# Context weights loaded one pair earlier, context projections ahead of the output blocks, and the gate's steps spread over later blocks

## The chip, the cores and the metric

The kernel runs on one core of a Trainium2 chip. The metric is the device time of one execution in microseconds; the time before is the median of three runs.

## The reference, cut to what matters

```
x = x + attn(layernorm(x))      # 16 heads of 64, causal, w_qkv and w_out
x = x + xattn(layernorm(x), ctx)
x = x + ffn(layernorm(x))       # x: 4 x 1024 x 1024, ctx: 4 x 1024 x 512
# xattn: query = ctx Wq^T + bq, key = ctx Wk^T + bk   (128 wide)
#        attention = softmax(query key^T);  x_m[l, m] = sum_n x[l, n] attention[m, n]
# ffn:   8 experts; u = select_weight . (x - mean_diff) / norm, score = sum u^2
#        gate = sigmoid(slope (score - center)); scale, index = max, argmax over the experts
#        out = (1 - scale) x + scale (bias[index] + degen[index] (update[index] . (x - debias[index])))
```

## The kernel before, in words

The batch has four sequences of 1024 rows. Each is done in eight head pairs, so there are 32 pairs n = 0 to 31 in one long software pipeline. Every 32-bit product is built out of three 16-bit products (high by high, high by low, low by high), which is why nearly each value has a high part, rounded on GpSimd or ScalarE, and a low part, made on VectorE. A row block is 128 rows, so a sequence has eight of them, 0 to 7.

The order of the work is written out by hand: for each engine there is a list of steps for a plain pair (PE_BODY and so on) and one for the last pair of a sequence (PE_TAIL and so on), which also carries everything that isn't attention. Every engine walks its own list in order, and a step that has to wait holds up all that stands behind it. A "+" behind a step means that it belongs to the next pair, or, for steps that aren't of a pair, to the next sequence; "-" means the pair before. The steps that matter here, with their lines:

- Attention of a pair. P (PE, L532 to L534): projections, four parts for each half of q, k and v. CH, CL (ACT L726, DVE L813): high and low part of a projection. S q (PE, L577): scores of row block q. X q (DVE, L846 to L853): row maxima. E q j (ACT, L739): exponential for head j. R q (DVE, L859, L862): reciprocal of the sum. H q j (POOL, L1077) and L q j (DVE, L813): high and low part of the probabilities. T q (SP, L418): DMA transpose of row block q, after L q 1. V (SP, L423): transpose of v. M g (PE, L602): probabilities times v for half g; M1 of a pair runs in the list of the next pair. OH, OL: high and low part of its result.
- Output projection. OI i (SP, L480): loads a quarter of w_out, 1 MB, into the room of the normalized x. B i h (PE): half h of output block i; B00 waits for all four OI of the sequence, B10 for RA0. RI i (SP, L499): x for the residual. RA i (DVE, L1040): adds the residual.
- Context. KI (SP, L485): the 512 KB of context weights, which go into the room of the attention weights. KH, KL (ACT L759, DVE L1005): their high and low part. JI i (SP, L491), JH i, JL i (ACT L766, DVE L1009): a quarter of the context and its two parts, through one buffer. G i (PE): its query and key; QH i, QL i (ACT L772, DVE L1018): the two parts of the result. N i, CX, CE, CR, CHI, CLO, CT: context scores, softmax and transpose.
- Cross attention and the gate, for row block i. LX, LH, LL, LT: second layer norm, its parts, its transpose. Z i h (PE): half h of x times attention. XB i (DVE, L1050): adds it. TB i (DVE, L818): statistics of the third norm; TS, TX, TH, TL, TT: that norm (ACT L797), its parts (DVE L1057) and transpose. F i (PE): gate and low-rank products. GA i (DVE, L936 to L950, 12 small instructions): scores of the experts. GE i (ACT, L801): exponential. GB i (DVE, L955 to L968, 8 small instructions and one over the whole block): choice of the expert, and the block scaled. D i (PE, L694), WHI i, WLO i (ACT L806, DVE L1064): transpose and parts of the low-rank row. U i (PE): up projection. Y i (DVE, L1069): sum; YO i (SP, L520): store.
- AI, AB, AS, AX, AH, AL, AT: first layer norm of the next sequence, between the steps of the gate.

The waits that the change touches or meets: F i waits for GB i-1 (the semaphore f_g, L687), D i for GB i, U i for WLO i and Y i-1, TX i for GB i-2 (two buffers of the normalized block, xn3), Z i for XB i-2, M1 of the last pair of a sequence for QL3 (L597), G 0 for KL and JL0, E of the first pair of a sequence for the last Y, H q for the transpose of q-2 (pn has two buffers), T0 to T3 for M1 of the pair before.

Of the kernel before, what the change touches and what calls it, by code (L numbers as in the profile page):

```python
# [137 lines left out]
def decoder_layer(nc, x, w_qkv, w_out, ctx_t, w_ctx, b_ctx, w_ffn, v_ffn, w_up, center, slope, out):  # L138
    es = ExitStack()
    with es:  # L140
# [66 lines left out]
        with ExitStack() as s1:  # L207
            sel_u = sb(s1, "sel_u", [P, EXPERTS * SEL])
            sel_sq = sb(s1, "sel_sq", [P, EXPERTS * SEL])
            g8 = sb(s1, "g8", [P, 12, EXPERTS])  # L210
            g1 = sb(s1, "g1", [P, 8])
# [999 lines left out]
```

## Time and profile before

| | |
|---|---|
| median of 3 runs | 2787.72 us (2785.35 to 2791.86) |
| the profiled execution | 2785.46 us, of which the span is 2783.6 us |
| TensorE (PE) busy | 2415.4 us, 87% of the span |
| VectorE (DVE) busy | 1877.4 us, 67% |
| ScalarE (ACT), GpSimd (POOL) busy | 783.4 us, 711.4 us |
| share of the chain that ended last | PE 52%, DVE 22%, DMA 12% |

TensorE is busy for most of the span. Times in rows are microseconds from the start of the span. In a row of the timeline the brackets say how long the engine was idle before the row, and what released it. The stretch from 1173.7 to 1497.5 is the list of the last pair of the second sequence (pair 15); the three other sequences have the same one, and that of the last sequence has no next sequence in it.

### The profile page before, as it was taken

What the parts mean: (1) busy time and instruction counts of PE and PEld (TensorE: products, weight loads), DVE (VectorE), ACT (ScalarE), POOL (GpSimd) and SP (SyncE); (2) the same over time, 40 slices, a digit from 0 to 9 for tenths busy, and PEclk for the clock granted to TensorE, in tenths of its full rate; (3) what the DMA queues carried; (4) which work ended last, traced back from release to release, by engine and by line L of the source; (5) the groups of instructions that cost most, each with busy time, mean ns of one, the idle gap of its engine ahead of it and who ended that gap; (6) DMA issues with size and microseconds to landing.
All of it is one profiled execution on the core that took longest, in us unless ns stands there. A gap on an engine that the chain in (4) does not pass through costs nothing.

```text
span 2783.6 us, 37859 instructions
## 1 busy us (share of the span) xinstructions
PE 2415.4 (87%) x14389; PEld 1187.7 (43%) x14389; DVE 1877.4 (67%) x3421; ACT 783.4 (28%) x1557; POOL 711.4 (26%) x981
## 2 busy tenths in 40 slices
PE   0588889699889999879979999979989999978996
PEld 0233444344444444445444444444444444434453
DVE  4577877646866767755785777765685777765566
ACT  1033333322213333321212333332211343332110
POOL 3123433214311222212421222212430222221220
PEclk9899999899999999989999999989989999998997
DMA  6678788857636776785654777776663677775543
GB/s 178 214 174 184 164 208 181 204 126 151 141 94 126 141 150 135 136 213 120 137 115 105 153 135 146 143 183 138 143 142 88 133 142 143 143 156 145 106 84 83
DMA packets 986009, 403.97 MB, mean 145 GB/s; under 512 B 937116, under 2 KB 946332, under 8 KB 985828
## 3 DMA queue, kind: packets, MB, share of 16 engines
q1 hardware_dynamic: 985828, 401.56, 65.3%
q8 instruction: 114, 1.87, 0.3%
q14 instruction: 67, 0.55, 0.1%
HBM read 133.05 MB, written 33.55 MB: 60 GB/s over the span
## 4 chain that ended last, share of the span: by engine, by line
PE 52%; DVE 22%; DMA 12%; issue 5%; ACT 4%; POOL 3%; SPq 2%; ACTq 0%; POOLq 0%; DVEq 0%
PE ps_p L532 8%; PE ps_p L534 8%; PE ps_p L533 8%; DMA r<-pn 7%; PE ps_s L532 5%; PE ps_s L533 5%; PE ps_s L534 5%; PE ps_s L577 5%; DVE pn L813 4%; PE ps_o L602 4%; DVE peak L850 3%; ACT probs L739 2%; DMA qk<-in_x 2%; DVE bn L818 2%; PE ps_s L582 1%
## 5 line engine op out<-in xcount | busy, mean ns | idle before, releaser
L1077 POOL TENSOR_SCALAR pn<-probs,rden 128x640 f16<-128x640 f32 (+7 forms) x512 | 386.6, 767 | 1297.0 <-DVE rden L862 830.4
L739 ACT ACTIVATE probs<-ps_s,low,back 128x640 f32<-128x640 f32 (+7 forms) x512 | 421.3, 826 | 859.0 <-DVE low L853 747.7
L813 DVE SCALAR_TENSOR_TENSOR pn<-probs,rden,pn 128x640 f16<-128x640 f32 (+7 forms) x512 | 473.9, 958 | 159.7 <-POOL pn L1077 159.5
L532 PE MATMUL ps_p<-r,w 128*128 128x512 f16 x1344 | 513.1, 382 | 3.3 <-DVE qk L813 3.3
L533 PE MATMUL ps_p<-r,w 128*128 128x512 f16 x1344 | 512.1, 381 | 0.0
L534 PE MATMUL ps_p<-r,w 128*128 128x512 f16 x1344 | 511.9, 381 | 0.0
L577 PE MATMUL ps_s<-qk 64*128 64x512 f16 (+3 forms) x2304 | 242.1, 336 | 129.5 <-ACT probs L739 122.8
L850 DVE TENSOR_REDUCE peak<-ps_s 128x2 f32<-128x1280 f32 (+3 forms) x128 | 241.3, 1885 | 36.6 <-PE ps_s L582 33.9
L602 PE MATMUL ps_o<-r,vn 128*64 128x512 f16 (+3 forms) x2304 | 212.2, 340 | 36.7 <-issue 36.1
L532 PE MATMUL ps_s<-r,pn 128*128 128x512 f16 x512 | 200.1, 391 | 11.0 <-DMA pn<-pn 11.0
L577 PEld LDWEIGHTS ps_s<-qk 64*128 64x128 f16 x2304 | 91.0, 96 | 274.0 <-ACT probs L739 171.6
L534 PEld LDWEIGHTS ps_p<-r,w 128*128 128x128 f16 x1344 | 132.2, 98 | 160.8 <-issue 4.2
L533 PE MATMUL ps_s<-r,pn 128*128 128x512 f16 x512 | 199.1, 389 | 0.0
L534 PE MATMUL ps_s<-r,pn 128*128 128x512 f16 x512 | 198.3, 387 | 0.0
L602 PEld LDWEIGHTS ps_o<-r,vn 128*64 128x64 f16 x2304 | 140.4, 114 | 125.2 <-issue 73.8
L532 PEld LDWEIGHTS ps_p<-r,w 128*128 128x128 f16 x1344 | 132.4, 99 | 141.8 <-DVE qk L813 5.3
L533 PEld LDWEIGHTS ps_p<-r,w 128*128 128x128 f16 x1344 | 132.4, 99 | 136.4 <-issue 2.5
L1081 POOL TENSOR_SCALAR ve<-mv 128x1 f32<-128x1 f32 x96 | 31.0, 323 | 473.0 <-DVE mv L821 471.5
L532 PE MATMUL ps_s<-r 128*128 128x512 f16 x384 | 145.9, 380 | 0.0
L533 PE MATMUL ps_s<-r 128*128 128x512 f16 x384 | 145.5, 379 | 0.0
L534 PE MATMUL ps_s<-r 128*128 128x512 f16 x384 | 145.5, 379 | 0.0
L859 DVE TENSOR_SCALAR den_s<-den 128x2 f32<-128x2 f32 x256 | 42.9, 167 | 133.9 <-ACT probs L739 133.6
(163 smaller groups left out, 3545.7 us busy)
## 6 DMA issues: line engine op xcount, KB each, us to landing
w<-w_pairs SPq DMA_DIRECT2D x72, 512.0 KB, 4.0
qk<-in_x SPq DMA_DIRECT2D x32, 512.0 KB, 4.2
r<-wo_pairs SPq DMA_DIRECT2D x16, 1024.0 KB, 6.1
w_raw<-in_x SPq DMA_DIRECT2D x32, 512.0 KB, 4.7
out<-r SPq DMA_DIRECT2D x32, 512.0 KB, 2.9
r<-in_w_qkv SPq DMA_DIRECT2D x24, 512.0 KB, 5.6
w_raw<-in_w_qkv SPq DMA_DIRECT2D x24, 512.0 KB, 5.7
w_pairs<-w SPq DMA_DIRECT2D x24, 512.0 KB, 5.5
```

Source lines behind the costliest of these rows:

```text
L532: pe.matmul(ps, lh, rh, start=start and k == ks[0], stop=False)
L533: pe.matmul(ps, lh, rl, start=False, stop=False)
L534: mm = pe.matmul(ps, ll, rh, start=False, stop=stop and k == ks[-1])
L577: pe.matmul(ps_s[:, j, to.start + c:to.start + d], qk_part(n, 0, qs, block_of(q))[rows(j), :], qk_part(n, 1, ks, slice(c, d))[rows(j), :], ...
L602: mm = pe.matmul(ps_o[rows(j), g, c:HALF], vn[:, n % 2, vs, kb, rows(j)], keys_of(g, j, s, kb), start=kb == 0 and vs == 0 and s == 0, stop ...
L739: act.activation(probs_part(q, j, w), ps_s[:, j, scores(q)], ACT.Exp, bias=low[:, n % 2, i:i + 1], scale=sc, accum_out=den[:, n % 2, i:i + ...
L813: dve.scalar_tensor_tensor(out=to, in0=bank, scalar=scale, in1=rounded, op0=ALU.mult, op1=ALU.subtract).then_inc(ok, 1)
L818: ins = dve.bn_stats(bn[:, T % 2, h, :], src[:, half(h)])
L850: dve.tensor_reduce(peak[:, n % 2, r], ps_s[:, :, scores(q)], AX_X, ALU.max).then_inc(peak_ok, 1)
L859: dve.tensor_scalar(den_s[:, n % 2, r], den[:, n % 2, r], 1.0 / UP_A, None, ALU.mult).then_inc(den_ok, 1)
L1077: pool.tensor_scalar(to, src, scale, 1.0, ALU.mult, ALU.mult).then_inc(ok, 1)
L1081: pool.tensor_scalar(ve, mv[:, 1:2], EPS, UP_X ** -2, ALU.add, ALU.mult).then_inc(ok_ve, 1)
```

## The change

It changes the lists for the last pair of a sequence, and a few buffers and waits that these need.

- KI leaves the head of SP_TAIL and is issued behind T6 of the seventh pair. OI1 now stands ahead of T0, and OI3 behind T4, JI2, RI0 and RI1. On ACT and DVE, KH stands behind E21, KL behind X3, X5 ahead of QL0 and JL1, L50 and L51 ahead of QL1 and JL2, and R7, RA0, L70, L71 ahead of QL2 and JL3. RA1 now stands ahead of QL3.
- On PE, G1 stands ahead of B00.
- F i stands behind Z(i+2)1, and D i and U i each one or two blocks later; on DVE, GA i stands behind TB(i+2), GB i ahead of TL(i+2), and Y i and WLO i follow. U7 and Y7 now stand behind S0 and S1 of the next sequence.
- Three rooms for the normalized block instead of two, two for low_h instead of one. The gate's scratch (s1) moves from under probs1 to under w_raw, so E no longer waits for the last Y, and the first RI of a sequence waits for the last Y of the sequence before.

```diff
 PE_TAIL = """
-    S2 S3 M1- S4 G0 S5 M0 S6 B00 G1 S7 B01 G2 B10 G3 B11 M1 B20 N0 B21 N1 B30 N2 B31 N3 B40 N4 B41 N5 B50 N6 B51 N7
-    B60 B61 B70 B71 Z00 Z01 Z10 Z11 Z20 F0 Z21 Z30 D0 Z31 U0 F1 Z40 Z41 D1 F2 Z50 U1 Z51 D2 F3 Z60 U2
-    D3 F4 Z61 U3 D4 Z70 U4 F5 Z71 D5 F6 P000+ P001+ P002+ P003+ U5 P010+ P011+ P012+ P013+ D6 P100+ P101+
-    P102+ P103+ U6 F7 P110+ P111+ P112+ P113+ P200+ P201+ D7 P202+ P203+ P210+ U7 P211+ P212+ P213+ S0+ S1+
+    S2 S3 M1- S4 G0 S5 M0 S6 G1 B00 S7 B01 G2 B10 G3 B11 M1 B20 N0 B21 N1 B30 N2 B31 N3 B40 N4 B41 N5 B50 N6 B51 N7
+    B60 B61 B70 B71 Z00 Z01 Z10 Z11 Z20 Z21 F0 Z30 Z31 F1 D0 Z40 Z41 F2 D1 U0 Z50 Z51 F3 D2 U1 Z60 Z61 F4 D3 U2
+    Z70 Z71 F5 D4 U3 P000+ P001+ P002+ P003+ P010+ P011+ P012+ P013+ F6 D5 U4 P100+ P101+ P102+ P103+ P110+ P111+
+    P112+ P113+ F7 D6 U5 P200+ P201+ P202+ P203+ P210+ P211+ P212+ P213+ D7 U6 S0+ S1+ U7
 """
 DVE_TAIL = """
-    X0 L70- L71- CL21 R0 X1 L00 L01 X2 R1 L10 L11 KL R2 X3 JL0 L20 L21 R3 OL1- X4 L30 L31 R4 QL0 JL1 X5 L40 L41
-    R5 OL0 X6 QL1 JL2 L50 L51 R6 X7 L60 L61 QL2 JL3 R7 RA0 L70 L71 QL3 RA1 LB0 OL1 CX0 LL0 LB1 CR0 RA2 CX1 CLO0
+    X0 L70- L71- CL21 R0 X1 L00 L01 X2 R1 L10 L11 R2 X3 KL L20 L21 OL1- R3 JL0 X4 L30 L31 R4 X5 QL0 JL1 L40 L41
+    R5 OL0 X6 L50 L51 QL1 JL2 R6 X7 L60 L61 R7 RA0 L70 L71 QL2 JL3 RA1 QL3 LB0 OL1 CX0 LL0 LB1 CR0 RA2 CX1 CLO0
     LB2 CR1 CX2 LL1 CLO1 CR2 RA3 CX3 CLO2 LB3 CR3 CX4 CLO3 CR4 RA4 CX5 CLO4 LB4 CR5 CX6 CLO5 CR6 RA5 CX7 CLO6 LB5
     CR7 CLO7 RA6 LB6 AB0+ AB1+ AL0+ RA7 LB7 AL1+
-    AB2+ XB0 TB0 LL2 AL2+ AB3+ TL0 LL3 XB1 TB1 AL3+ AB4+ GA0 GB0 TL1 LL4 XB2 TB2 AL4+ AB5+ WLO0 GA1 TL2 GB1
-    LL5 XB3 TB3 Y0 AL5+ AB6+ WLO1 GA2 TL3 GB2 LL6 XB4 TB4 Y1 AL6+ AB7+ WLO2 GA3 TL4 GB3 LL7 XB5 TB5 Y2 AL7+
-    WLO3 GA4 TL5 GB4 XB6 Y3 TB6 WLO4 GA5 TL6 GB5 Y4 XB7 WLO5 TB7 GA6 GB6 Y5 TL7 CL00+ CL01+ WLO6 GA7 CL10+
-    GB7 Y6 CL11+ CL20+ WLO7 Y7 CL21+
+    AB2+ XB0 TB0 LL2 AL2+ AB3+ TL0 LL3 XB1 TB1 AL3+ AB4+ TL1 LL4 XB2 TB2 GA0 AL4+ AB5+ GB0 TL2 LL5 XB3 TB3 GA1
+    WLO0 AL5+ AB6+ GB1 TL3 LL6 XB4 TB4 GA2 WLO1 Y0 AL6+ AB7+ GB2 TL4 LL7 XB5 TB5 GA3 WLO2 Y1 AL7+ GB3 TL5 XB6 TB6
+    GA4 WLO3 Y2 GB4 TL6 XB7 TB7 GA5 WLO4 Y3 GB5 TL7 CL00+ CL01+ GA6 WLO5 Y4 GB6 CL10+ CL11+ GA7 WLO6 Y5 GB7 CL20+
+    WLO7 Y6 CL21+ Y7
 """
 ACT_TAIL = """
-    E00 E01 CH21 E10 E11 KH E20 E21 JH0 E30 E31 OH1- E40 E41 QH0 JH1 E50 E51 OH0 E60 E61 QH1 JH2 E70 E71 QH2 JH3
+    E00 E01 CH21 E10 E11 E20 E21 KH E30 E31 JH0 OH1- E40 E41 QH0 JH1 E50 E51 OH0 E60 E61 QH1 JH2 E70 E71 QH2 JH3
     QH3 LX0 OH1 CE0 LX1 CE1 CE2 CE3 LX2 CE4 CE5 CE6 CE7 AX0+ AX1+ AX2+ TX0 LX3 AX3+ TX1
-    LX4 AX4+ GE0 TX2 WHI0 LX5 AX5+ GE1 TX3 WHI1 LX6 AX6+ GE2 TX4 WHI2 LX7 AX7+ GE3 TX5 WHI3 GE4 TX6 WHI4
-    GE5 WHI5 TX7 GE6 CH00+ CH01+ WHI6 CH10+ GE7 CH11+ CH20+ WHI7 CH21+
+    LX4 AX4+ TX2 GE0 LX5 AX5+ TX3 GE1 WHI0 LX6 AX6+ TX4 GE2 WHI1 LX7 AX7+ TX5 GE3 WHI2 TX6 GE4 WHI3 TX7 GE5 WHI4
+    CH00+ CH01+ GE6 WHI5 CH10+ CH11+ GE7 WHI6 CH20+ WHI7 CH21+
 """
 POOL_TAIL = """
     H00 H01 H10 H11 H20 H21 H30 H31 H40 H41 H50 H51 H60 H61 H70 H71 LS0 LH0 CHI0 LS1 CHI1 LH1 LS2 CHI2 CHI3 LS3
@@ -84,10 +84,10 @@
     AH6+ TS4 AS7+ TH4 LH7 AH7+ TS5 TH5 TS6 TH6 TS7 TH7
 """
 SP_TAIL = """
-    OI0 KI JI0 T0 OI1 T1 OI2 T2 JI1 T3 OI3 T4 JI2 RI0 RI1 T5 JI3 T6 T7 WD0+ WD1+ WD2+ RI2 RI3 CT0 LT0 CT1 RI4
+    OI0 JI0 OI1 T0 T1 OI2 T2 JI1 T3 T4 JI2 RI0 RI1 OI3 T5 JI3 T6 T7 WD0+ WD1+ WD2+ RI2 RI3 CT0 LT0 CT1 RI4
     LT1 RI5 CT2 CT3 RI6 CT4 CT5 RI7 CT6 CT7 AI0+ AI1+ AI2+ AT0+ AT1+ AI3+ LT2 AT2+
-    TT0 AI4+ LT3 AT3+ TT1 AI5+ LT4 AT4+ AI6+ TT2 LT5 YO0 AT5+ AI7+ TT3 LT6 YO1 AT6+ TT4 LT7 YO2 AT7+ TT5
-    YO3 TT6 YO4 TT7 YO5 WD0++ YO6 WD1++ YO7 V+
+    TT0 AI4+ LT3 AT3+ TT1 AI5+ LT4 AT4+ AI6+ TT2 LT5 AT5+ AI7+ TT3 LT6 YO0 AT6+ TT4 LT7 YO1 AT7+ TT5
+    YO2 TT6 YO3 TT7 YO4 WD0++ YO5 WD1++ YO6 V+ YO7
 """
...
+for pair in range(PAIRS - 2, BATCH * PAIRS, PAIRS):
+    ONCE["SP", pair, "T6"] = "KI"
...
-            low_h = sb(s1, "low_h", [P, GK])
+            low_h = sb(s1, "low_h", [P, 2, GK])
...
+        def norm3(i):
+            return xn3[:, i % 3, :] if i % 3 < 2 else w_raw[:, 1, :]
...
                             sp.wait_ge(w_ok, 3 * PAIRS)
                         else:
-                            sp.wait_ge(x1_ok, TB * b)
+                            sp.wait_ge(y_ok, TB * b)
...
-                            if b > 0:
-                                act.wait_ge(y_ok, TB * b)
...
-                        if i >= 2:
-                            act.wait_ge(f_x, T - 1)
+                        if i >= 3:
+                            act.wait_ge(f_x, T - 2)
                         else:
                             act.wait_ge(n_mm, TB * (b + 1))
-                        act.activation(xn3[:, i % 2, :], x1[:, i, :], ACT.Identity, bias=sh3[:, i:i + 1],
+                        act.activation(norm3(i), x1[:, i, :], ACT.Identity, bias=sh3[:, i:i + 1],
                                        scale=rs3[:, i:i + 1]).then_inc(d_xn, 1)
```

## Rows read from the trace of the kernel before

**Rows 1.** Busy time by stretch: us, PE, PEld, DVE, ACT, POOL, PEclk, DMA share, GB/s.

```profile
1173.70:1251.30 77.60, 53.27 (x338) 31.04 (x340) 40.69 (x68) 22.65 (x44) 11.72 (x16) 0.85 0.84 203
1251.30:1372.20 120.90, 120.86 (x602) 59.35 (x601) 80.69 (x132) 24.79 (x30) 42.29 (x66) 1.00 0.59 128
1372.20:1497.50 125.30, 104.26 (x575) 56.93 (x575) 85.48 (x215) 21.87 (x37) 24.62 (x39) 0.93 0.49 115
2682.30:2780.60 98.30, 73.27 (x416) 42.27 (x414) 70.31 (x191) 11.27 (x21) 12.51 (x23) 0.86 0.36 86
```

**Rows 2.** Waits of PE, whole span: us in total, times, longest us.

```profile
PE ps_p L532 <- DVE r L1040: 28.2, 4, 7.5
PE ps_p L532 <- DVE lt_lo L1064: 23.8, 12, 3.9
PE ps_o L694 <- DVE low_h L966: 22.5, 11, 4.5
```

**Rows 3.** Timeline of PE: start us, us; S4, B10 and M1 of pair 15.

```profile
1195.90 1.78 PE L577 MATMUL ps_s<-qk 64*128 64x512 f16 x12 [7.78 <-ACT probs L739]
...
1235.84 0.61 PE L532 MATMUL ps_p<-r 128*128 128x512 f16 x1 [7.01 <-DVE r L1040]
...
1251.26 0.41 PE L602 MATMUL ps_o<-r,vn 128*64 128x512 f16 x2
```

**Rows 4.** Timeline of ACT: KH of the second sequence.

```profile
1189.97 1.06 ACT L759 ACTIVATE wc_hi<-wc_raw 128x1024 fp32r<-128x1024 f32 x1 [11.96 <-DMA wc_raw<-in_w_ctx]
```

**Rows 5.** Timeline of SP, issues: T0, OI1, T4 (at L41's end), RI0 with RI1.

```profile
1188.20 1.22 SPq L418 DMA_TRANSPOSE r<-pn  x1
1189.46 0.59 SPq L480 DMA_DIRECT2D r<-wo_pairs  x1
...
1208.67 3.07 SPq L418 DMA_TRANSPOSE r<-pn  x1
...
1212.42 1.11 SPq L499 DMA_DIRECT2D w_raw<-in_x  x2
```

**Rows 6.** Timeline of POOL: H20 with H21, H30 with H31.

```profile
1192.83 1.14 POOL L1077 TENSOR_SCALAR pn<-probs,rden 128x384 f16<-128x384 f32 x2 [9.79 <-DVE rden L862]
1196.89 1.36 POOL L1077 TENSOR_SCALAR pn<-probs,rden 128x512 f16<-128x512 f32 x2 [2.92 <-DMA r<-pn]
```

**Rows 7.** Busy time by stretch, columns as in rows 1: loads behind T4; start of B10.

```profile
1210.00:1215.00 5.00, 5.00 (x31) 2.18 (x28) 2.94 (x3) 1.81 (x4) 1.43 (x2) 1.00 1.08 240
...
1235.80:1240.10 4.30, 4.26 (x11) 1.50 (x12) 3.32 (x2) 0.00 (x0) 1.09 (x1) 0.50 0.00 0
```

**Rows 8.** Part 6 of the page, OI: KB each, median us from issue to landing.

```profile
r<-wo_pairs SPq DMA_DIRECT2D x16, 1024.0 KB, 6.1
```

**Rows 9.** Timeline of DVE: QL3 and RA1.

```profile
1247.04 0.88 DVE L1018 SCALAR_TENSOR_TENSOR qk_lo<-ps_o,bias_c,qk_hi 128x256 fp32r<-128x256 f32 x2 [7.89 <-ACT qk_hi L772]
1251.37 1.28 DVE L1040 SCALAR_TENSOR_TENSOR r<-ps_p,back,w_raw 128x1024 f32<-128x1024 f32 x1 [3.45 <-PE ps_p L534]
```

**Rows 10.** Timeline of DVE: within GA2; GB5's ends; XB7; GA6's ends.

```profile
1398.16 0.97 DVE L948 TENSOR_TENSOR g<-g,center_b 128x8 f32<-128x8 f32 x1
...
1450.10 0.16 DVE L955 TENSOR_SCALAR g<-g 128x8 f32<-128x8 f32 x1
...
1451.72 1.28 DVE L968 SCALAR_TENSOR_TENSOR r<-xn,g,r 128x1024 f32<-128x1024 f32 x1
...
1454.05 1.21 DVE L1050 SCALAR_TENSOR_TENSOR r<-ps_s,r 128x1024 f32<-128x1024 f32 x1
...
1456.82 0.23 DVE L936 SCALAR_TENSOR_TENSOR sel_u<-ps_o,back,ffn_c 128x64 f32<-128x64 f32 x1
...
1459.09 0.28 DVE L950 SCALAR_TENSOR_TENSOR low_h<-ps_o,back,ffn_c 128x64 f32<-128x64 f32 x1
```

**Rows 11.** Waits of DVE from 1372.2 to 1497.5, columns as in rows 2.

```profile
DVE sel_u L936 <- PE ps_o L534: 16.8, 3, 6.6
```

**Rows 12.** Timeline of PE: S2 of the third sequence.

```profile
1497.52 0.66 PE L577 MATMUL ps_s<-qk 64*128 64x384 f16 x6 [1.22 <-ACT probs L739]
```

More of the change, by code:

```diff
@@ L206, in decoder_layer @@
         cn = xh1 = probs0[:, :].bitcast(F16).rearrange("p (s h d) -> p s h d", s=2, h=2)
[L207 to L211, printed above, removed]
-            low_h = sb(s1, "low_h", [P, GK])
-            lt_hi = sb(s1, "lt_hi", [GK, P], F32R)
-            lt_lo = sb(s1, "lt_lo", [GK, P], F32R)
         probs1 = sb(es, "probs1", [P, 2 * SEQ])
@@ L221, in decoder_layer @@
         t2 = pn[:, 1, :].rearrange("p (s h k t) -> p s h k t", s=2, h=2, k=KC)
+        with ExitStack() as s1:
+            sel_u = sb(s1, "sel_u", [P, EXPERTS * SEL])
+            sel_sq = sb(s1, "sel_sq", [P, EXPERTS * SEL])
+            g8 = sb(s1, "g8", [P, 12, EXPERTS])
+            g1 = sb(s1, "g1", [P, 8])
+            low_h = sb(s1, "low_h", [P, 2, GK])
+            lt_hi = sb(s1, "lt_hi", [GK, P], F32R)
+            lt_lo = sb(s1, "lt_lo", [GK, P], F32R)
         w_raw = sb(es, "w_raw", [P, 2, KC * P])
@@ L316, in walk @@
                         for once, which, _ in steps(ONCE.get((engine, n, kind + "".join(map(str, args))), "")):
-                            rest(once, which, 0)
+                            rest(once, which, n // PAIRS)
         def rows(j):
@@ L693, in rest @@
                             pe.wait_ge(ll_ok, T)
-                        pe.transpose(ps_o[0:GK, 1, 0:P], low_h[:, :], ident[:, :]).then_inc(l_turn, 1)
+                        pe.transpose(ps_o[0:GK, 1, 0:P], low_h[:, i % 2, :], ident[:, :]).then_inc(l_turn, 1)
                     elif kind == "U":
@@ L949, in gate_scores @@
                     dve.tensor_tensor(g8[:, 4, :], g8[:, 2, :], slope_b[:, :], ALU.mult).then_inc(f_z, 1)
-                    dve.scalar_tensor_tensor(out=low_h[:, 0:64], in0=ps[:, 64:128], scalar=c_ffn, in1=ffn_c[:, 64:128],
+                    dve.scalar_tensor_tensor(out=low_h[:, i % 2, 0:64], in0=ps[:, 64:128], scalar=c_ffn, in1=ffn_c[:, 64:128],
                                              op0=ALU.mult, op1=ALU.subtract)
@@ L961, in gate_choice @@
                     gate_step(dve.tensor_reduce(g1[:, 3:4], g8[:, 8, :], AX_X, ALU.max), T, 13)
-                    dve.tensor_scalar(low_h[:, 64:GK], g8[:, 8, :], g1[:, 3:4], g1[:, 2:3], ALU.is_equal,
+                    dve.tensor_scalar(low_h[:, i % 2, 64:GK], g8[:, 8, :], g1[:, 3:4], g1[:, 2:3], ALU.is_equal,
                                       ALU.mult).then_inc(f_w, 1)
                     dve.wait_ge(f_w, T + 1)
-                    lh = low_h[:, 0:64].rearrange("p (n h) -> p n h", h=LOW)
-                    dve.tensor_tensor(lh, lh, low_h[:, 64:GK].unsqueeze(2).broadcast_to([P, EXPERTS, LOW]),
+                    lh = low_h[:, i % 2, 0:64].rearrange("p (n h) -> p n h", h=LOW)
+                    dve.tensor_tensor(lh, lh, low_h[:, i % 2, 64:GK].unsqueeze(2).broadcast_to([P, EXPERTS, LOW]),
                                       ALU.mult).then_inc(f_g, 1)
-                    dve.scalar_tensor_tensor(out=x1[:, i, :], in0=xn3[:, i % 2, :], scalar=g1[:, 4:5], in1=x1[:, i, :],
+                    dve.scalar_tensor_tensor(out=x1[:, i, :], in0=norm3(i), scalar=g1[:, 4:5], in1=x1[:, i, :],
                                              op0=ALU.mult, op1=ALU.add).then_inc(f_x, 1)
@@ L1056, in rest @@
                         dve.wait_ge(d_hi, T + 1)
-                        dve.tensor_tensor(xh3[:, 1, :], xn3[:, i % 2, :], xh3[:, 0, :], ALU.subtract).then_inc(d_lo, 1)
+                        dve.tensor_tensor(xh3[:, 1, :], norm3(i), xh3[:, 0, :], ALU.subtract).then_inc(d_lo, 1)
                     elif kind == "GA":
@@ L1151, in rest @@
                             pool.wait_ge(t3_in, 16 * T)
-                        rounded(xh3[:, 0, :], xn3[:, i % 2, :], 1.0, d_hi)
+                        rounded(xh3[:, 0, :], norm3(i), 1.0, d_hi)
                 pool.memset(ones[:, :], 1.0)
```

## The prediction

> **What bounds the kernel now.** I read the busy times by stretch first [rows 1]. In the last pair of the second sequence TensorE is full between 1251.3 and 1372.2 (120.86 of 120.90 us), so nothing is to be had there. The context and output stage ahead of it has 24.3 us without TensorE (77.60 - 53.27), the gate stage behind it 21.0 (125.30 - 104.26), and the last sequence's gate, which has no next sequence to fill it, 25.0. Then the waits of PE [rows 2]: 28.2 us in four waits, one per sequence, for RA0 (the residual ahead of B10), 23.8 for WLO and 22.5 for GB. These 74.5 us are what the change can remove; a further cost hangs on them, the slow clock behind a wait: after 7.01 us idle B10 ran its first 4.3 us at a granted clock of 0.50, the lower level (1.2 GHz) [rows 3, 7]. At half speed half of these 4.3 us is lost, about 2 us.
>
> In the gate stage the engine that is late is VectorE: 85.48 us busy, but it also waits 16.8 us for F (L936) [rows 1, 11]. It is neither full nor free, a ring in which PE, DVE and ACT wait for each other in turn.
>
> **The context weights.** KH waited 11.96 us for KI and held up E20, and with it S4, 7.78 us [rows 3, 4]. With KI a pair earlier this wait goes, and S4 can follow M1. What is late next is the low part L20, on VectorE, ahead of JL0 (for which G0 waits) and X4. L20 needs H20, and H20 needs the transpose T0 landed, which waits for M1. Before, T0 was issued at 1188.20, ahead of OI1 at 1189.46 [rows 5]; now OI1 (1 MB) is ahead of it. How such a place costs is shown by T1, which stood behind OI1: H30 began at 1196.89 only, released by that transpose [rows 6]. I expect T0 to land about 1195, H20 to begin there instead of at 1192.83, and X4 to end about 0.6 us later than before, in spite of the earlier E20. So the 7.78 us before S4 turn into as many before G0: worth nothing. Bounds per sequence: -3 (T0 lands as before) to +3 (KI's 512 KB also push back T7, and M1 with it; at the 240 GB/s of rows 7 they are 2.2 us).
>
> **OI3 and B00.** B00 waits for all four quarters of w_out. L41 ends where T4 is issued, at 1208.67 [rows 5]; in the new order X5 comes ahead of QL0 and JL1, but L40 behind these, so L41 ends about where it did: I take +0.9 (0.6 from X4, the rest from the order). T4 takes 3.1 us of SP, then come JI2 (0.6) and both RI (1.1) [rows 5], and only then OI3, issued about 1214.5. Ahead of it in the queue lie 1.5 MB, and its own 1 MB: 2.62 million bytes at 240 GB/s [rows 7] are 10.9 us from the end of T4 at 1212.7, so it lands about 1224 (1220.5 if it took the median of 6.1 us of an OI from its issue [rows 8]; 1227 if its reads start only behind the others and 3 us are lost). B00 started at 1210.9, just before G1. G1 (3.2 us) now fills a part of this; PE stands idle some 9 us, S7 is behind it, and B00 loses 2 us to the clock. On the other side RA0 is no longer behind JL3, whose load came late, and R7 follows L61: RA0 is done about 6.7 us after S7, while B01 and G2 take 8.3, so the 7.01 us before B10 go. The sum for the end of B10: OI3 at 1224, B00 5.35 + 2, S7 1.6, B01 5.2, G2 3.1, B10 5.35 = 1246.6, against 1243.3 before (1235.84 + 7.4 [rows 3]): +3.3. The other three sequences worked the same way from their own L41 give +1.5 to +3.9; I take +12.3 for the four. Bounds per sequence: -7 (the load is in time and only the gain stays) to +7 (1227 and the T0 bound).
>
> By the Trainium skill (DMA: Bandwidth & Descriptors, section Queues, rings and completion order) each DMA engine consumes the descriptors of a ring in the order in which they were put there. By that OI3 waits for the 1.5 MB ahead, and the sum is the one above; were it not so, the median would hold, and the four sequences would lose about 14 us less. H30's release agrees with the rule.
>
> **QL3 behind RA1.** M1 of pair 15 waits for QL3. Before, QL3 was done at 1247.9, ahead of B11's end, and M1 followed B11 at once (1251.26) [rows 3, 9]. Now QL3 stands behind RA1, and RA1 waits for B11. So M1 waits 1.28 + 0.88 and two hand-overs, 2.4 us, in each sequence: +9.6. Nothing covers it: B20 stands behind M1. Bounds +2.0 to +3.5 (the M1 begins slower).
>
> **The gate.** Up to XB7 VectorE now does one GA, one GB, one WLO and two Y less (they come beside the next projections): 2.6 + 2.9 + 0.3 + 2.4 = 8.2 us (first to last row of GA6 and of GB5 [rows 10]; 1.2 for a Y, a full-block pass as L1050). The waits for F shrink, since F i now stands a block ahead of GA i. Against it: GB i now stands behind AB(i+4), where GpSimd has AS, TH, LH and AH to do, which before stood beside GA. A small step that meets one of these takes 0.97 us (L948 in GA2) [rows 10], where it takes 0.17 free; GA2 had 1.7 us in all from that. I move that sum to GB. WLO i stands right behind GA(i+1) on DVE, but WHI i behind GE(i+1), so each WLO waits 0.5. And PE: F(i+1) waits for GB i, 3 to 4 us behind the end of Z(i+2). That is idle of PE, but Z(i+3) is still done some 7 us before its XB, so the ring isn't closed by it. Walked through step by step with these durations, XB7 starts at 1437 instead of 1454.05 [rows 10]. Behind it stand F5, U3, the 24 parts of projection (31 us), F6, F7, four U, and at the end a chain: D7, U6, Y6, CL21, S0, S1, U7, Y7, X0, E00, S2, with about 5 us idle of PE where there were 2.6. S2 comes 50 us behind XB7's start, at 1487.8 to 1489; it was at 1497.52 [rows 12]. I take -8.5 in each of three sequences, -25.5; bounds -13 (no contention in GB) to -2 (each GB full of it, and waits of F that close the ring). In the last sequence nothing of the next stands beside the gate, the period is that of PE (Z 10.4, F 1.4, U 1.6), and only the tail after TB7 is left as a chain: 98.3 us shrink to about 88, -10 (bounds -5 to -14).
>
> By the Trainium skill (SBUF — State Buffer, section Who interferes with whom) a VectorE instruction with two SBUF inputs and a GpSimd one that reads SBUF exclude each other for the whole instruction. The row of 0.97 agrees. If every GpSimd step that now falls into a GB stopped it whole (three of 1.04 us each), GB would take 1.4 us more than I take, and the gate's three stages would give about 12 us less: the estimate would be -1.6 us in all.
>
> Rooms and waits: the third room lets TX3 go after GB0 instead of GB1, already in the walk. E's wait for the last Y is gone; nothing waited there before. RI0 waits for the last Y of the sequence before, done long ago. All nothing.
>
> **Sum.** +12.3 + 9.6 - 25.5 - 10 = -13.6 us. The profiled execution took 2785.46 us (span 2783.6), so it would take about 2771.9; the median of the runs lies 2.3 above that execution, at 2787.7. Prediction: 2774 us.
>
> **Rivals.** (1) Slower: the ring of the gate closes. F(i+1) behind Z(i+2)1 waits for GB i, and Z(i+3) stands behind F; if GB is later than in my walk by more than the 7 us that Z has in hand, XB(i+3) waits for Z and the period is that of the longer chain GB, F, Z, XB. Then the three stages give nothing and the last 5: +22 - 5 = 2805. For it: PE already waits 22.5 us for GB. Against it: 7 us in hand. (2) The halves cancel: contention in GB as by a full lock and OI3 at 1227: within 5 us of before, 2788. For it: both are costs that I took low. (3) OI3 is in time, as L41 comes earlier than I think: the 28.2 us of RA0 and 8 of clock go, less 9.6 for QL3, less the gate's 35.5: 2726. For it: E20 is 12 us earlier. Against it: T0 behind OI1, and 2.6 million bytes behind T4. (4) KI isn't earlier at all, as it waits for the last projection part of the seventh pair: but that part is done by 1173.7, where the first stretch of rows 1 begins, 16 us before KH; I give it nothing.
>
> **Chances.** Forecast 0.52 (its own range 2757 to 2783), (1) 0.17, (2) 0.21, (3) 0.10. A measurement of this kernel can tell about 0.2% (5.6 us) from no change, so faster is below 2782, slower above 2793. Faster: 0.50 + 0.10 + 0.03 = 0.63; within 0.2%: 0.18; slower: 0.19. Range for 8 in 10: 2744, which takes in a part of (3), to 2803.
>
> **What would show it.** PE waiting 7 to 12 us before B00 for r<-wo_pairs, in all four sequences, and no wait for L1040 before B10. M1 of the last pairs waiting 2 to 3 us. S4 at once behind M1, and G0 waiting instead. XB7 at 15 to 18 us earlier within its gate stage, waits of PE for L966 of 3 to 4 us before F2 and F3, and GB near 4.7 us there. The prediction is wrong if B00 doesn't wait, or if the stage from 1372 to the next S2 isn't 5 us shorter.

## The result, and the profile after

The changed kernel took 2772.5 us, median of 5 runs (2768.79 to 2775.5), beside 2787.72 (2785.35 to 2791.86) for the kernel before: a ratio of 0.9941, 95% interval 0.9926 to 0.9955. Predicted were 2774, a ratio of 0.9951. The profiled execution has a span of 2770.6 us (before 2783.6), PE busy 2404.3, DVE 1884.6, ACT 782.0, POOL 717.5.

Steps keep their names below; the line numbers of the changed kernel are 3 to 5 higher (matmul L537 to L539, scores L582, M L607, D L699, GB's last two steps L969 and L971, TL L1060).

Busy time by stretch, changed kernel, columns as in [rows 1], whose first four rows the first four of these answer to (S2 of pair 15 to its own M1, a stretch of full TensorE, gate stage up to the next S2, gate of the last sequence); then two thirds of B00 and the 3 us of U7:

```profile
1168.80:1253.40 84.60, 53.60 (x338) 32.01 (x339) 41.78 (x70) 22.62 (x44) 12.65 (x16) 0.82 0.78 193
1253.40:1376.00 122.60, 122.36 (x600) 60.08 (x600) 77.07 (x124) 27.16 (x32) 43.73 (x68) 0.99 0.61 128
1376.00:1491.40 115.40, 102.75 (x576) 55.40 (x576) 90.15 (x222) 18.95 (x35) 23.18 (x36) 0.93 0.51 119
2679.70:2767.60 87.90, 71.43 (x416) 42.79 (x413) 68.12 (x191) 10.89 (x22) 12.37 (x22) 0.85 0.42 96
1219.90:1222.90 3.00, 2.97 (x8) 1.07 (x9) 0.00 (x0) 0.00 (x0) 0.00 (x0) 0.50 1.10 261
1222.90:1225.90 3.00, 3.00 (x9) 1.07 (x8) 0.00 (x0) 0.00 (x0) 0.00 (x0) 0.50 0.30 104
1485.50:1488.50 3.00, 2.92 (x8) 1.82 (x6) 0.04 (x1) 0.00 (x0) 0.00 (x0) 0.50 1.08 232
```

Nearly the same matmul records stand in each stretch as before (x338, x600 for x602, x576 for x575). The first stretch grew by 7.0 us (77.60 to 84.60), 6.7 of it time without TensorE; the third shrank by 9.9 (125.30 to 115.40) and the fourth by 10.4 (98.30 to 87.90), and in both VectorE is fuller.

Waits of PE over the whole span, changed kernel, columns as in [rows 2]:

```profile
PE ps_s L582 <- ACT probs L742: 97.9, 82, 3.5
PE ps_p L537 <- issue: 42.8, 4, 11.2
PE ps_o L537 <- DVE low_h L969: 38.0, 14, 5.9
PE ps_o L537 <- DVE ctx_lo L1012: 33.2, 4, 8.9
PE ps_o L607 <- DVE qk_lo L1021: 9.0, 4, 2.3
```

Of the three waits of [rows 2] those for RA0 and for WLO are gone from the view. In their place stand B00's four for OI3 (42.8; the profile names no releaser, the landing below does), F's for GB (38.0), G0's for the context's low part JL0 (33.2) and M1's for QL3 (9.0).

Timeline of PE in the last pair of the second sequence, changed kernel: G0, B00, M1 (brackets: idle before, releaser):

```profile
1193.33 0.58 PE L537 MATMUL ps_o<-ctx_hi,wc_hi 128*128 128x256 f32 x1 [8.25 <-DVE ctx_lo L1012]
...
1219.93 0.59 PE L537 MATMUL ps_p<-r 128*128 128x512 f16 x1 [11.19 <-issue]
...
1253.38 5.99 PE L607 MATMUL ps_o<-r,vn 128*64 128x512 f16 x48 [2.25 <-DVE qk_lo L1021]
```

SP's issues there, changed kernel: OI1, then T0 with T1 behind it, T3 with T4, JI2, both RI, and OI3 only then ([rows 5] have T0 ahead of OI1):

```profile
1181.24 0.63 SPq L485 DMA_DIRECT2D r<-wo_pairs  x1
...
1184.03 2.70 SPq L423 DMA_TRANSPOSE r<-pn  x2
...
1196.29 12.61 SPq L423 DMA_TRANSPOSE r<-pn  x2
1208.95 0.58 SPq L496 DMA_DIRECT2D vt<-in_ctx_t  x1
1209.58 1.09 SPq L504 DMA_DIRECT2D w_raw<-in_x  x2
1210.71 0.53 SPq L485 DMA_DIRECT2D r<-wo_pairs  x1
```

The landing of that OI3, from the view of the DMAs issued between 1210 and 1212 (KB, us from issue to landing):

```profile
r<-wo_pairs SPq DMA_DIRECT2D x1, 1024.0 KB, 9.1
```

It landed at 1219.8, and B00 began at 1219.93.

The context weights came less early than the title of the change says. KI waits for the last projection part of the seventh pair, so SP issued it only with the start of S2:

```profile
1168.75 0.34 SPq L490 DMA_DIRECT2D wc_raw<-in_w_ctx  x1
```

Counted from S2 that is 9.4 us sooner than in the kernel before (1183.05 - 1173.7), and not a whole pair. It was enough that KH no longer waits for it.

The end of the gate stage. The first rows of S0, U7 and S2 on PE, changed kernel; S2 answers to [rows 12]:

```profile
1484.44 0.34 PE L582 MATMUL ps_s<-qk 64*128 64x128 f16 x6 [2.47 <-DVE vt L816]
...
1485.52 0.78 PE L537 MATMUL ps_p<-up_hi,lt_hi 72*128 72x512 f32 x1
...
1491.42 1.14 PE L582 MATMUL ps_s<-qk 64*128 64x384 f16 x6 [3.00 <-ACT probs L742]
```

To see where time went in all four sequences, I read the start of each last pair's S2 and of each Z00 from the timelines. "Front" is S2 to Z00, "gate" is Z00 to the next S2, "pairs" the seven pairs between, "last" Z00 of the fourth sequence to the end of PE's work. Sums in us, single profiled executions:

```
                                  front x4  gate x3  pairs x3  last
before                              624.8    502.2    994.6   140.0
after                               646.2    475.6    998.0   129.6
e1 OI3 ahead of T4                  598.0    475.5    998.2   129.6
e2 QL3 ahead of RA1                 636.8    475.1    998.9   129.6
e3 gate only                        629.4    476.3    999.4   129.6
e4 front only                       647.3    500.4    996.8   141.7
e5 KI back                          646.0    478.0    999.4   129.6
e6 OI3, QL3                         584.6    478.0    999.7   129.6
e7 OI3, QL3, T0                     585.9    480.4    998.3   129.3
e8 e7, tail mended                  580.5    471.3    995.7   127.6
e9 e8, KI back                      581.5    465.3    994.9   127.6
e10 e8, GB free                     582.3    456.1    992.6   127.6
e11 e9, GB free                     579.5    454.7    993.3   127.5
e12 e9, OI2 later                   591.2    464.9    996.2   127.9
```

The change lost 21.4 in the fronts and 3.4 in the pairs, and won 26.6 in the gates and 10.4 in the last: -12.2. With the 0.9 by which its first S2 came earlier that is the difference of the spans, -13.0.

### The profile page after: what moved, and what is told of

It is laid out like the page before. It is cut to its first block, busy times and chain, and to the rows that moved or that the text cites. A ratio compares the mean times of both kernels' runs of the same rounds, so it can differ in the third digit from the quotient of the medians.

```text
span 2770.6 us, 37859 instructions
## 1 busy us (share of the span) xinstructions
PE 2404.3 (87%) x14389; PEld 1186.3 (43%) x14389; DVE 1884.6 (68%) x3421; ACT 782.0 (28%) x1557; POOL 717.5 (26%) x981
## 4 chain that ended last, share of the span: by engine, by line
PE 59%; DVE 19%; DMA 10%; issue 6%; ACT 3%; POOL 2%; SPq 1%; ACTq 0%; POOLq 0%; DVEq 0%
PE ps_p L537 8%; PE ps_p L538 8%; PE ps_p L539 8%; DMA r<-pn 8%; PE ps_s L537 6%; PE ps_s L538 6%; PE ps_s L539 6%; PE ps_s L582 6%; PE ps_o L607 5%; DVE pn L816 4%; DVE peak L853 3%; ACT probs L742 2%; DVE bn L821 2%; DMA qk<-in_x 2%; PE ps_s L587 1%
## 5 line engine op out<-in xcount | busy, mean ns | idle before, releaser
L537 PE MATMUL ps_p<-r,w 128*128 128x512 f16 x1344 | 515.1, 383 | 3.1 <-DVE qk L816 3.1
L539 PE MATMUL ps_p<-r,w 128*128 128x512 f16 x1344 | 513.7, 382 | 0.0
L582 PE MATMUL ps_s<-qk 64*128 64x512 f16 (+3 forms) x2304 | 239.0, 332 | 107.9 <-ACT probs L742 97.9
L607 PE MATMUL ps_o<-r,vn 128*64 128x512 f16 (+3 forms) x2304 | 210.9, 339 | 39.3 <-issue 30.0
L539 PEld LDWEIGHTS ps_p<-r,w 128*128 128x128 f16 x1344 | 132.5, 99 | 162.1 <-issue 6.3
L582 PEld LDWEIGHTS ps_s<-qk 64*128 64x128 f16 x2304 | 90.0, 95 | 252.3 <-ACT probs L742 147.4
L537 PE MATMUL ps_s<-r,pn 128*128 128x512 f16 x512 | 195.6, 382 | 0.0
L538 PE MATMUL ps_s<-r,pn 128*128 128x512 f16 x512 | 195.2, 381 | 0.0
L607 PEld LDWEIGHTS ps_o<-r,vn 128*64 128x64 f16 x2304 | 141.1, 113 | 126.2 <-issue 76.7
L539 PE MATMUL ps_s<-r,pn 128*128 128x512 f16 x512 | 195.0, 381 | 0.0
L537 PEld LDWEIGHTS ps_p<-r,w 128*128 128x128 f16 x1344 | 132.8, 99 | 142.8 <-DVE qk L816 5.1
L537 PE MATMUL ps_s<-r 128*128 128x512 f16 x384 | 145.9, 380 | 0.0
L539 PE MATMUL ps_s<-r 128*128 128x512 f16 x384 | 145.5, 379 | 0.0
L862 DVE TENSOR_SCALAR den_s<-den 128x2 f32<-128x2 f32 x256 | 42.8, 167 | 133.3 <-ACT probs L742 133.3
```

The costliest lines, as they stand in the source:

```text
L537: pe.matmul(ps, lh, rh, start=start and k == ks[0], stop=False)
L538: pe.matmul(ps, lh, rl, start=False, stop=False)
L539: mm = pe.matmul(ps, ll, rh, start=False, stop=stop and k == ks[-1])
L582: pe.matmul(ps_s[:, j, to.start + c:to.start + d], qk_part(n, 0, qs, block_of(q))[rows(j), :], qk_part(n, 1, ks, slice(c, d))[rows(j), :], ...
L607: mm = pe.matmul(ps_o[rows(j), g, c:HALF], vn[:, n % 2, vs, kb, rows(j)], keys_of(g, j, s, kb), start=kb == 0 and vs == 0 and s == 0, stop ...
L862: dve.tensor_scalar(den_s[:, n % 2, r], den[:, n % 2, r], 1.0 / UP_A, None, ALU.mult).then_inc(den_ok, 1)
```

## The experiments

Ratios are to the kernel before, measured anew beside each group of kernels. "After" is the changed kernel. Lists that don't change are left out of the diffs.

**e1: OI3 ahead of T4.** Is B00's wait the load's place in the queue?

```diff
-OI0 JI0 OI1 T0 T1 OI2 T2 JI1 T3 T4 JI2 RI0 RI1 OI3 T5
+OI0 JI0 OI1 T0 T1 OI2 T2 JI1 T3 OI3 T4 JI2 RI0 RI1 T5
```

> The changed kernel with one step moved: OI3 is issued behind T3, ahead of T4. My theory: the load lands before G1 ends, so the four waits of B00 for it (42.8 us in the changed kernel's profile) and the half clock behind them (8.6 us over four B00) go, and no wait comes in their place, as RA0 no longer stands behind JL3: 51 us less than the changed kernel, about 2721. The rival: B00 would be early, but then B10 waits for RA0 as before the change, 5 to 7 us per sequence: about 2745. A second rival, that B00 waited for something else: no change, 2772.

2725.35 us, ratio 0.9772 (0.9757 to 0.9786). All waits of PE in that last pair, e1, up to B10:

```profile
1163.89 0.82 PE L582 MATMUL ps_s<-qk 64*128 64x512 f16 x6 [3.50 <-ACT probs L742]
1168.53 6.17 PE L607 MATMUL ps_o<-r,vn 128*64 128x512 f16 x48 [3.60 <-issue]
1185.12 0.58 PE L537 MATMUL ps_o<-ctx_hi,wc_hi 128*128 128x256 f32 x1 [9.28 <-DVE ctx_lo L1012]
1193.16 1.82 PE L607 MATMUL ps_o<-r,vn 128*64 128x512 f16 x24 [1.83 <-issue]
1195.54 1.31 PE L582 MATMUL ps_s<-qk 64*128 64x512 f16 x12 [0.56 <-ACT probs L742]
```

No row for B00 nor for B10 is left: the theory held, 4 us short of its 51. The load's place costs 47 us, 42.8 of idle and the rest mostly the slow clock behind it; it is worth three times the whole change.

**e2: QL3 ahead of RA1.**

```diff
-RA0 L70 L71 QL2 JL3 RA1 QL3 LB0
+RA0 L70 L71 QL2 JL3 QL3 RA1 LB0
```

> The changed kernel with QL3 ahead of RA1 on VectorE. My theory: M1 of the last pair of a sequence no longer waits for QL3 behind RA1 (4 x 2.25 us), and the one of these four M1 that ran at half clock behind it is fast again: 9 to 11 us less than the changed kernel, about 2762, with no wait left at that place. The rival: RA1 is late then by QL3 and N0, which waits for it, pays: N0 stands behind M1 and B20 (10 us), so I give it nothing; if it were so, the gain would be under 3 us.

2761.41, ratio 0.9901 (0.9886 to 0.9916), -11 us against after; the four waits for QL3 (9.0) are gone, each of the four M1 takes 4.41 us, and B00's waits (39.2) stay. The theory held.

**e3 and e4: the halves apart.** e3 has the new gate (lists from the first XB on, rooms, waits) behind the old front; e4 the reverse.

```diff
 e3, SP:  OI0 KI JI0 T0 OI1 T1 OI2 T2 JI1 T3 OI3 T4 JI2 ...   (as before)
 e3, PE:  ... S6 B00 G1 S7 ... Z20 Z21 F0 Z30 Z31 F1 D0 ...   (new from Z20 on)
 e4, SP:  OI0 JI0 OI1 T0 T1 OI2 T2 JI1 T3 T4 JI2 RI0 RI1 OI3  (as after)
 e4, PE:  ... S6 G1 B00 S7 ... Z20 F0 Z21 Z30 D0 Z31 U0 ...   (old from Z20 on)
```

> Only the part of the change behind M1 of a sequence's last pair (the gate's steps spread, three rooms, U7 and Y7 at the end); the lists ahead of it and KI's place as before the change. My theory: the gate gives all of the gain, 26.6 us in the first three sequences and 10.4 in the last, less 3.6 in the first pair behind: 33 to 37 us less than the kernel before, about 2752. The rival: the gate stage only gives back what the earlier part lost (it starts late and catches up), then it gives less than 20 us by itself: about 2770.

2757.04, ratio 0.9882 (0.9868 to 0.9896): -31.7 against the kernel before measured beside it (2788.72), 1 to 5 less than the 33 to 37 expected. PE's waits in the old front, e3, S4 and B10:

```profile
1190.62 1.78 PE L582 MATMUL ps_s<-qk 64*128 64x512 f16 x12 [7.02 <-ACT probs L742]
...
1232.65 0.61 PE L537 MATMUL ps_p<-r 128*128 128x512 f16 x1 [6.87 <-DVE r L1043]
```

> Only the part of the change up to QL3 of a sequence's last pair (KI in the seventh pair, T0 behind OI1, OI3 behind RI1, G1 ahead of B00, RA1 ahead of QL3); the gate's lists as before the change (its three rooms stay, and give nothing by themselves). My theory: this part costs 21 us (4.0, 8.6, 6.0 and 2.8 us per sequence between the profiles): about 2809. The rival: it is neutral, as the gate stage behind it has waits that absorb a late start: about 2788.

2808.77, ratio 1.0065 (1.0052 to 1.0078): +20. The halves add up: -31.7 + 20.1 = -11.6, where both together gave -15.2. By the table e3's gain is 25.9 in the gates and 10.4 in the last, less some 9 in fronts and pairs.

**e5: KI back.** The changed kernel with KI behind OI0 of the last pair again.

```diff
-OI0 JI0 OI1 T0 T1
+OI0 KI JI0 OI1 T0 T1
```

> The changed kernel with KI alone put back behind OI0 at the head of the last pair's list; KH and KL stay behind E21 and X3. My theory: KI's early issue is worth next to nothing in this change, since L20 waits for the transpose T0, which lands behind OI1 (20.2 us after S2 in the changed kernel), later than KI would (16 us after S2): 0 to 6 us more than the changed kernel, 2772 to 2778. The rival: the early KI is what keeps the context stage going (KH waited 12 us for it before), then 4 x 5 us or more are lost: 2792 or more.

2777.01, ratio 0.9954 (0.994 to 0.9969), whose interval holds after's 0.9941. The waits before G0 fell from 33.2 to 19.1, while S4 waited 3.4 to 5.9 for the exponentials again, and the fronts came out equal (646.0 and 646.2). KI's early load moved a wait from S4 to G0 and gained nothing.

**e6 and e7: both front mends, then T0 and T1 ahead of OI1.**

```diff
 e6, SP:
-OI0 JI0 OI1 T0 T1 OI2 T2 JI1 T3 T4 JI2 RI0 RI1 OI3 T5
+OI0 JI0 OI1 T0 T1 OI2 T2 JI1 T3 OI3 T4 JI2 RI0 RI1 T5
 e7, SP:
+OI0 JI0 T0 T1 OI1 OI2 T2 JI1 T3 OI3 T4 JI2 RI0 RI1 T5
 both, DVE: QL3 ahead of RA1, as e2
```

> The changed kernel with two moves: the load OI3 right behind the transpose T3, ahead of T4, and the low part QL3 ahead of the residual RA1 on VectorE. It is the kernel of e7 without T0 and T1 ahead of OI1. Theory (the two moves are independent, since one removes waits ahead of B00 and the other one ahead of M1): alone they gave 0.9772/0.9941 and 0.9901/0.9941 against the changed kernel, so together 0.9732 of the kernel before, about 2714, and no wait of PE for OI3 nor for L1021. By that T0 ahead of OI1 was worth 4 to 6 us in e7 and not 11. Rival (in a kernel where B00 no longer waits, M1 is set by something else than QL3, and QL3's move gives nothing): about 2724, the time of e1.

2715.28, ratio 0.9744 (0.9728 to 0.9759); theory 0.9732, rival 0.9772 (e1's ratio), which the interval leaves out. The mends add up.

> The changed kernel with OI3 ahead of T4, QL3 ahead of RA1, and OI1 behind T0 and T1. By the two kernels measured singly the first two give 47 + 11, so 2714 without the third. My theory: T0 no longer lands behind OI1's 1 MB, so L20, JL0, G0 and X4 come some 3 us earlier in each sequence: 12 us less, about 2703, and PE's wait for L1012 before G0 falls from 9 to 6 us. The rival: the transfers behind (T2, JI1, T3) are then as much later, as the queue is full there: about 2714.

2708.69, ratio 0.9715 (0.9696 to 0.9734), between the two. The wait before G0 fell to 23.3, but T2, JI1 and T3 now stood behind two loads of 1 MB, and M0 came no earlier. The fronts of e6 and e7 are equal (584.6 and 585.9) and their intervals touch: whether T0's place is worth anything isn't settled.

**e8: the end of the gate stage mended.** U7 and Y7 go back ahead of S0.

```diff
 PE:
-P200+ P201+ P202+ P203+ P210+ P211+ P212+ P213+ D7 U6 S0+ S1+ U7
+P200+ P201+ P202+ P203+ U6 P210+ P211+ D7 P212+ U7 P213+ S0+ S1+
 DVE:
-GB7 CL20+ WLO7 Y6 CL21+ Y7
+GB7 Y6 CL20+ WLO7 Y7 CL21+
 SP:
-YO6 V+ YO7
+YO6 YO7 V+
```

> As the one with T0 ahead, and at the end of the gate U6, D7 and U7 between the projection parts, Y6 ahead of CL20 and Y7 ahead of CL21, so that X0 of the next sequence stands behind nothing of the gate. My theory: the chain U6, Y6, CL21, S0, S1, U7, Y7, X0 costs 1 us before S0, 2 before S2, 1.3 by U7 at half clock and 2 by the slow first steps of the next pair, in three sequences: 18 us less than the one before it, about 2685, and the first pair of a sequence no longer 1 to 2 us longer. The rival: D7 and U7 wait inside the projection instead and the gain is under 6 us: about 2699.

2698.48, ratio 0.9666 (0.9645 to 0.9686): 10 us less than e7 by the medians, 14 by the ratios. That lies between the theory's 18 and the rival's "under 6", and neither is confirmed; the rival's 2699 was counted from the 2703 that e7 was expected to take. S0 and S2 on PE, e8:

```profile
1455.57 0.34 PE L582 MATMUL ps_s<-qk 64*128 64x128 f16 x6 [1.42 <-DVE vt L816]
...
1458.00 1.14 PE L582 MATMUL ps_s<-qk 64*128 64x384 f16 x6 [1.22 <-ACT probs L742]
```

From S0 to S2 it is 2.4 us, where the changed kernel took 7.0. Against e7 the three gates are 9.1 us shorter and the pairs 2.6.

**e9: e8 with KI back.**

```diff
-OI0 JI0 T0 T1 OI1 OI2 T2
+OI0 KI JI0 T0 T1 OI1 OI2 T2
```

> As the one with the end of the gate mended, but KI back behind OI0. My theory: with T0 ahead of OI1 the context weights are the later of the two at L20 and JL0, as KH starts only when KI has landed some 16 us after S2, and JI0 stands behind it: 4 to 10 us more than with KI early. The rival: still nothing, within 3 us.

2693.06, ratio 0.9649 (0.9628 to 0.967): a miss, it is not slower (nor surely faster: the intervals overlap). The fronts are equal to 1 us, as in e5. The 6 us less in its gates are not of the edit, as the lists there are the same; they are TensorE's clock. Busy time by stretch in the second gate, columns as in [rows 1], first e8, then e9, and XB7 of the same gate in both:

```profile
1379.00:1389.00 10.00, 8.67 (x39) 5.80 (x40) 9.79 (x15) 1.24 (x1) 4.84 (x6) 0.50 0.54 101
1379.00:1389.00 10.00, 8.71 (x58) 5.15 (x59) 9.79 (x15) 1.24 (x1) 4.83 (x7) 1.00 0.55 102
1411.35 1.23 DVE L1053 SCALAR_TENSOR_TENSOR r<-ps_s,r 128x1024 f32<-128x1024 f32 x1 [2.30 <-PE ps_s L539]
1408.62 1.22 DVE L1053 SCALAR_TENSOR_TENSOR r<-ps_s,r 128x1024 f32<-128x1024 f32 x1 [0.39 <-PE ps_s L539]
```

Around PE's wait for GB ahead of F3 (3.55 us in e8, 2.10 in e9) the granted clock stood at 0.50 for 10 us in e8 and not in e9; the Z behind it came late, XB7 waited for it, and the gate took 3.2 us more. All three gates of e8 have this stretch, one of e9's. Of the 30 gates of the kernels with the new gate (without e10 and e11) nine have it, 10 us around F3: XB7 stands 109.9 to 110.8 us behind Z00 in these and 106.6 to 107.9 in the others. No edit accounts for them: with equal gate lists the changed kernel has none, e5 one and e7 two. So some 3 us per such gate are to be taken off before two profiles are compared.

**e10 and e11: GpSimd's steps out of GB.** On VectorE AB5, AB6, AB7 go behind GB0, GB1, GB2, and on GpSimd AS5, AS6, AS7 just ahead of AH5, AH6, AH7, in e8 and in e9.

```diff
 DVE:
-AL4+ AB5+ GB0 TL2 ... AL5+ AB6+ GB1 TL3 ... AL6+ AB7+ GB2 TL4
+AL4+ GB0 AB5+ TL2 ... AL5+ GB1 AB6+ TL3 ... AL6+ GB2 AB7+ TL4
 POOL:
-TS2 AS5+ TH2 LH5 AH5+ TS3 AS6+ TH3 LH6 AH6+ TS4 AS7+ TH4 LH7 AH7+
+TS2 TH2 LH5 AS5+ AH5+ TS3 TH3 LH6 AS6+ AH6+ TS4 TH4 LH7 AS7+ AH7+
```

> The kernel of e8 (tail mended) with the GpSimd steps that fall into GB0, GB1 and GB2 moved: on VectorE AB5, AB6, AB7 stand behind GB0, GB1, GB2 instead of ahead of them, and on GpSimd AS5, AS6, AS7 stand just ahead of AH5, AH6, AH7. Theory (the small steps of GB are held up by GpSimd's steps beside them): GB0 to GB2 fall from 4.4 to about 2.9 us, PE's waits for GB (L969, 37.1 us in e8) fall to about 25, and the time by 8 to 12 us against e8: 2687 to 2690, ratio 0.963. Rival (the GpSimd steps only move into GA, TL or WLO, and the ring of gate and attention keeps its period): GB is shorter but others longer by as much, time within 4 us of e8, about 2698.

> The same move of the GpSimd steps in the kernel of e9, which loads the context weights KI behind OI0 in the last pair again. Theory: as much less against e9 as e10 is against e8 (8 to 12 us), so 2681 to 2685, ratio 0.961. Rival: within 4 us of e9, about 2693.

2680.46, ratio 0.9622 (0.9609 to 0.9635), and 2678.26, ratio 0.9613 (0.96 to 0.9626). Against e8 and e9 these are 12 and 10 us less by the ratios, 18 and 15 by the medians, where 8 to 12 were expected. The last two steps of GB2 and the TL4 behind them, VectorE, e8:

```profile
1379.19 1.00 DVE L969 TENSOR_TENSOR low_h<-low_h 128x64 f32<-128x64 f32 x1
1380.11 2.08 DVE L971 SCALAR_TENSOR_TENSOR r<-w_raw,g,r 128x1024 f32<-128x1024 f32 x1
1382.12 2.05 DVE L1060 TENSOR_TENSOR vn<-xn,vn 128x1024 f16<-128x1024 f32 x1
```

and in e10:

```profile
1366.00 0.23 DVE L969 TENSOR_TENSOR low_h<-low_h 128x64 f32<-128x64 f32 x1
1366.14 1.28 DVE L971 SCALAR_TENSOR_TENSOR r<-w_raw,g,r 128x1024 f32<-128x1024 f32 x1
...
1368.78 1.17 DVE L1060 TENSOR_TENSOR vn<-xn,vn 128x1024 f16<-128x1024 f32 x1
```

0.77, 0.80 and 0.88 us less in one block, 2.45 together. GB2 fell from 4.44 to 2.89, GB1 to 3.73; GB0 stayed (4.53). PE's waits for GB fell from 37.1 to 31.4 us, not to the 25 expected. Not all of the gain is GB's: the 10 us at a granted clock of 0.50 stand in all three gates of e8 and in none of e10 or e11 (one of e10's has 7 us of it). Between gates of e9 and e11 without it XB7 comes 2.1 to 3.0 us earlier, some 8 us in three gates, and that is the move's own price. Whether the shorter waits also kept the clock up isn't shown.

**e12: OI2 behind JI1, in e9.**

```diff
-OI0 KI JI0 T0 T1 OI1 OI2 T2 JI1 T3 OI3
+OI0 KI JI0 T0 T1 OI1 T2 JI1 OI2 T3 OI3
```

> The kernel of e9 with the load OI2 behind the load JI1 instead of behind OI1, so that the transpose T2 has 1 MB less ahead of it in SP's queue. Theory (a transpose that stands behind loads in the queue lands late, and the attention chain of the last pair pays it): T2 lands 2 to 3 us earlier, the waits of PE for probs in the last pairs fall, and the time by 4 to 8 us against e9: 2685 to 2689. Rival (the bytes ahead of T3 and OI3 stay the same and these land as late or later, so that OI3 comes late and B00 waits for it again): 0 to 6 us slower than e9, 2693 to 2699, with a wait of PE in front of B00.

2700.08, ratio 0.9692 (0.9679 to 0.9705): slower than e9 by 7 (medians) to 12 us (ratios), 9.7 of them in the fronts. T2 did land sooner (3.7 us after its issue instead of 6.5). But T3 now had OI2 right ahead of it. The transposes' landing (us) and M0 on PE, e9:

```profile
r<-pn SPq DMA_TRANSPOSE x1, 5.6
```

```profile
1188.11 1.82 PE L607 MATMUL ps_o<-r,vn 128*64 128x512 f16 x24 [1.62 <-issue]
```

and e12:

```profile
r<-pn SPq DMA_TRANSPOSE x1, 8.0
```

```profile
1185.57 3.41 PE L607 MATMUL ps_o<-r,vn 128*64 128x512 f16 x24 [4.21 <-issue]
```

M0 needs T3, which landed at 1188.0 in e9 and 1185.3 in e12 (issue and landing added), just ahead of M0; but S2 stood 5.3 us earlier in e12, so M0 came 2.8 late. The rival was right that T3 lands later and that the time grows; but there was no wait before B00, and neither theory named T3 as what M0 waits for.

## Why the prediction came out right

The sum was -13.6 us on the profiled execution and the spans differ by -13.0. The signs and the sizes of all four terms were right, but that the sums meet within 1 us is in part luck: single terms were off by up to 3.4 us, both ways, and the walk through the gates left out some 10 us of cost that something else made up for (below). Its steps:

- **OI3 and B00, predicted +12.3, measured +10.8: right.** For pair 15, from S2: OI3 predicted to land at 50.3 us (1224 - 1173.7), landed at 51.0 (1219.8 - 1168.8), issued 1.1 later than predicted and landing 9.1 us after its issue instead of 9.5; B00 predicted 7.35 us long, measured 8.28, since it ran at 0.50 for 6.0 us and not for the 4.3 of [rows 7]; the end of B10 +4.7 instead of +3.3. M1 stands 4.0, 7.0, 6.0, 2.8 later behind S2 in the four sequences; without QL3's 2.25 each, +10.8. e1 shows the cause.
- **QL3 behind RA1, predicted +9.6: right.** Measured 9.0 of wait, and 1.6 of clock in one M1 (5.99 us where the others took 4.41). e2 gave -11.
- **Context weights, worth nothing: right.** S4 followed M1 at once and G0 waited 8.25; e5 and e9 show it by undoing. (What KI gained was 9 us and not a pair; rival (4) came half true, as KI did wait for that projection part.)
- **The gate, predicted -25.5: right in its sum (-26.6).** XB7 stands 107.9 us behind Z00 instead of 125.0, 17.2 earlier (walk: 17), and the chain from XB7 to S2 took 50.8 (walk: 50). GB was 4.44 us in GB0 to GB2 (predicted near 4.7) and 2.9 from GB3 on. PE's waits for GB stood before F1, F2 and F4 (3.62, 2.18, 1.36), not before F2 and F3.
- **The last gate, predicted -10: measured -10.4.**
- **Missed: +3.4 in the pairs behind the gate.** U7 and the first 4 to 5 us of the next pair run at a granted clock of 0.50 (1.2 GHz), between and behind waits of 2.47 and 3.00 us; before the change it was the first 3 us of that pair, in two of three sequences; I had counted the chain's waits and not this. In e8, without the chain, the pairs are 2.3 shorter than after.

Rival (1), the closed ring, did not come: Z stays ahead, as walked. Rival (2) did not either: GB took 4.44 us and not 6, and OI3 landed within 1 us of the forecast. Rival (3), OI3 in time, is e1, which took 2725 where I had worked out 2726.

What held up [rows 10] in small steps now shows in GB. VectorE's last two steps of GB1, changed kernel, with the TL3 behind them:

```profile
1394.10 1.01 DVE L969 TENSOR_TENSOR low_h<-low_h 128x64 f32<-128x64 f32 x1
1395.03 2.09 DVE L971 SCALAR_TENSOR_TENSOR r<-xn,g,r 128x1024 f32<-128x1024 f32 x1
1397.04 2.05 DVE L1060 TENSOR_TENSOR vn<-xn,vn 128x1024 f16<-128x1024 f32 x1
```

and GpSimd beside them, changed kernel:

```profile
1393.99 1.05 POOL L1080 TENSOR_SCALAR vn<-xn 128x1024 f16<-128x1024 f32 x1
1395.00 1.05 POOL L1080 TENSOR_SCALAR pn<-pn 128x1024 f16<-128x1024 f32 x1
```

L969 ends with the first GpSimd step (1395.11 and 1395.04), L971 ends 1.07 us behind the end of the second (1396.05). The Trainium skill (SBUF — State Buffer, section Who interferes with whom) has it that a VectorE instruction with two SBUF inputs contends with a GpSimd one that reads SBUF, that their shared port pair is an exclusive lock, and that issue order decides who blocks. This trace agrees: the VectorE steps are 0.78 and 0.81 us longer. I had carried the stop as one sum of 1.7 us into GB (measured: 1.55) and none into TL, where it costs another 0.84 a block: TL1 to TL4 take 2.05 instead of 1.22 (TL0 did so before the change too), 3.3 us in each of the three gates. There was no slack for it: between 33 and 102 us behind Z00 VectorE waits nowhere for more than 0.45 us in the changed kernel. XB7 came where the walk had it all the same, so some other term of the walk was too high by about as much; which one isn't shown.

The best version measured is e11, 0.9613 (0.96 to 0.9626) of before, though its interval doesn't part it from e10's: the new gate, with OI3 and QL3 put right, the end mended, GB free, and the context weights where they were.
